# Graph attention layer: neighbouring groups of edges share their scores, their maximum and their exponentials

## What is computed

```python
h = einsum('ni,hio->hno', x, W)                       # rows of 256, and two scores of 4 per node
e = attn_src[:, src_idx] + attn_dst[:, dst_idx]
e = where(e >= 0, e, 0.2 * e) * edge_weight
e_exp = exp(e - max(e))
denom = segment_sum(e_exp, dst_idx)
out = segment_sum(h[:, src_idx] * e_exp / (denom[:, dst_idx] + 1e-10), dst_idx)
```

## Time and profile before

| | us |
|---|---|
| median of 3 runs (range) | 2468.64 (2465.61 to 2472.03) |
| the profiled execution | 2466.78 |
| its span | 2465.0 |
| start of the gathers of layer 1, from the span's start | 1695.59 |

### The profile page before, as it was taken

How to read it: one execution, slowest core, us unless ns; L and a number is a source line. 1 busy time by engine, 2 the same in 40 slices (tenths; PEclk the granted TensorE clock), 3 DMA queues, 4 the chain that set the end, 5 groups by cost and what they waited for, 6 DMA issues and landing times.

```text
span 2465.0 us, 41568 instructions
## 1 busy us (share of the span) xinstructions
PE 1989.2 (81%) x12990; PEld 1757.5 (71%) x12990; DVE 1594.8 (65%) x4240; ACT 1416.0 (57%) x2926; POOL 1473.5 (60%) x1204
## 2 busy tenths in 40 slices
PE   7799999999999999999999999945155655555560
PEld 6699889999999999989999989943144444444450
DVE  6466666666666666666666666654266566666575
ACT  2488888888888888888888888834011111111112
POOL 0327777777776777767777777423555555555503
PEclk9899999999999999999999999977567767776785
DMA  6888877777777777777777777574344544444413
GB/s 209 282 208 184 193 165 164 167 163 170 159 158 155 161 158 158 159 157 160 158 160 158 160 159 156 112 186 126 91 113 121 128 112 118 119 119 115 120 48 108
DMA packets 236177, 370.91 MB, mean 150 GB/s; under 512 B 35853, under 2 KB 168935, under 8 KB 235949
## 3 DMA queue, kind: packets, MB, share of 16 engines
q0 software_dynamic: 101232, 188.20, 38.7%
q1 hardware_dynamic: 134717, 179.94, 24.7%
HBM read 270.57 MB, written 97.45 MB: 149 GB/s over the span
## 4 chain that ended last, share of the span: by engine, by line
PE 56%; issue 18%; DVE 11%; ACT 5%; DMA 5%; another core or an unknown queue 4%; POOL 1%; SPq 0%; DVEq 0%; ACTq 0%; POOLq 0%
PE bank L1412 12%; PE bank L1410 12%; PE bank L1411 12%; PE bank L1462 4%; PE bank L1453 4%; DMA accA<-ystage,to_a 3%; PE bank L1479 2%; DVE in_window L860 2%; PE bank L1503 2%; PE bank L1514 2%; PE bank L1504 2%; PE bank L1515 2%; PE bank L1578 1%; ACT drop L1849 1%
## 5 line engine op out<-in xcount | busy, mean ns | idle before, releaser
L1306 POOL DMA_INDIRECT accA<-ystage,to_a x391 | 649.7, 1662 | 233.8 <-issue 111.6
L1312 POOL DMA_INDIRECT GA<-TA,src_c x391 | 426.7, 1091 | 323.3 <-issue 95.4
L1341 POOL DMA_INDIRECT Hg<-HT,src_c x391 | 372.9, 954 | 335.6 <-DVE xb L912 174.8
L1849 ACT ACTIVATE drop<-neg_m 128x1 f32<-128x1 f32 x98 | 28.9, 295 | 613.1 <-issue 348.2
L1410 PE MATMUL bank<-h1h,W1h 128*128 128x512 f32 x882 | 349.2, 396 | 1.5 <-DVE h1l L536 1.4
L1412 PE MATMUL bank<-h1h,W1l 128*128 128x512 f32 x882 | 348.3, 395 | 0.0
L1411 PE MATMUL bank<-h1l,W1h 128*128 128x512 f32 x882 | 347.3, 394 | 0.0
L536 DVE TENSOR_TENSOR h2l<-h2f,h2h 128x512 fp32r<-128x512 f32 (+1 forms) x294 | 202.9, 690 | 202.6 <-issue 78.9
L1607 PE MATMUL bank<-diag,ones 128*128 128x128 f32 x196 | 66.5, 435 | 306.3 <-DVE diag L896 250.2
L1617 PE MATMUL bank<-xb,in_window 128*128 128x260 f32 (+1 forms) x782 | 292.9, 542 | 1.1 <-issue 1.1
L536 DVE TENSOR_TENSOR h1l<-h1f,h1h 128x512 fp32r<-128x512 f32 x294 | 195.1, 691 | 131.3 <-ACT h1h L1686 114.2
(11 more groups left out here) (208 smaller groups left out, 5196.0 us busy)
## 6 DMA issues: line engine op xcount, KB each, us to landing
TW<-TB SPq DMA_DIRECT2D x196, 203.0 KB
ef<-in_eT SPq DMA_DIRECT2D x97, 256.0 KB
bcast_i<-in_src_row SPq DMA_DIRECT2D x97, 256.0 KB
HB<-hist SPq DMA_DIRECT2D x98, 130.0 KB
rel<-RL SPq DMA_DIRECT2D x97, 128.0 KB
rem<-RD SPq DMA_DIRECT2D x48, 256.0 KB
TB<-stB SPq DMA_DIRECT2D x24, 406.0 KB
accA<-zeros SPq DMA_DIRECT2D x4, 1677.0 KB, 13.1
```

Of the source, the lines that this page charges most:

```text
L1306: return pool.indirect_dma_start(out=table, out_offset=bass.IndirectOffsetOnAxis(ap=rows, axis=0), in_=sums, in_offset=None, compute_op=AL ...
L1312: pool.indirect_dma_start(out=GA[0:n, b % (GAR * BLOCKS_PER_GROUP), :].bitcast(f32), out_offset=None, in_=TA, in_offset=bass.IndirectOffse ...
L1341: pool.indirect_dma_start(out=Hg[0:n, slot, :], out_offset=None, in_=HT, in_offset=bass.IndirectOffsetOnAxis(ap=src_c[0:n, b:b + 1], axis= ...
```

## The change

Two neighbouring groups become a pair q of NQ = 49 pairs. One-hot matrix, scores, diagonal, spread, running maximum, `drop` and exponentials are made once for a pair, on tiles twice as wide, and `window_rows` is too. Weighing, sums, carry and store stay one for each group; the odd group of a pair is carried with `keep` alone. The ring `xb` grows from 3 to 4 groups, `hist` shrinks from 8 to 6. PAD has one bank in place of two, PTOP one in place of two, PS three in place of four, and the weights have two banks for themselves. VectorE's order in iteration q is now: weigh 2q, carry 2q-2, maximum q+1, weigh 2q+1, carry 2q-1, scores q+2, window q+1, one-hot q+3. TensorE's is: sums 2q and 2q+1, spread q+2, destination scores q+3. A part of the diff (the other functions are rewritten for pairs in the same way):

```diff
...
-        REMG = 2
-        rem = sb("rem", [P, 2, REMG * GE], bf16, s2)
-        HOTR = 4
-        hot = sb("hot", [P, HOTR, GE], bf16, s2)
-        XBR = 3
-        xb = sb("xb", [P, XBR, BLOCKS_PER_GROUP, BW], f32, s2)
-        in_window = sb("in_window", [P, XBR, BLOCKS_PER_GROUP, P], f32, s2)
+        rem = sb("rem", [P, 2, 2 * GE], bf16, s2)
+        hot = sb("hot", [P, 2, 2 * GE], bf16, s2)
+        XBR = 4
+        xb = sb("xb", [P, XBR * BLOCKS_PER_GROUP, BW], f32, s2)
+        in_window = sb("in_window", [P, XBR * BLOCKS_PER_GROUP, P], f32, s2)
         diag = sb("diag", [P, 2, P], f32, s2)
...
-        HISTR = 8
+        HISTR = 6
...
-        PAD, PTOP, PS = bank[0:2], bank[2:4], bank[4:8]
+        PAD, PTOP, PS = bank[0], bank[1], bank[5:8]
...
-        iota_p, node_p = bank[2][:, P:2 * P], bank[3][:, P:P + NT * HEADS].rearrange("p (t h) -> p t h", h=HEADS)
-        GH = BLOCKS_PER_GROUP * HEADS
-
-        def weight_p(g):
-            return bank[2][:, 2 * P + g % XBR * GH:2 * P + (g % XBR + 1) * GH].rearrange("p (k h) -> p k h", h=HEADS)
+        iota_p, node_p = bank[2][:, 0:P], bank[2][:, P:P + NT * HEADS].rearrange("p (t h) -> p t h", h=HEADS)
+        QH = 2 * BLOCKS_PER_GROUP * HEADS
+
+        def weight_p(q):
+            return bank[3 + q % 2][:, 0:QH].rearrange("p (k h) -> p k h", h=HEADS)
...
+            def one_hot(q):
+
+                n = edges_of_group(2 * q) + edges_of_group(2 * q + 1)
+                dve.wait_ge(s_rem[q % 2], 16 * (q // 2 + 1))
+                if q >= 2:
+                    dve.wait_ge(s_ad, q - 1)
+                dve.tensor_scalar(hot[:, q % 2, 0:n], rem[:, q % 2, 0:n], p_f[:, :], None, ALU.is_equal).then_inc(s_hot, 1)
+
...
+            def window_rows(q):
+
+                if q >= 2:
+                    dve.wait_ge(s_S, 2 * (q - 1))
...
+            def edge_scores(q):
+
+                blocks = blocks_of_window_pair(q)
                 runs = same_rows(blocks)
-                dve.wait_ge(s_hg[g % HGR], group_arrivals(HGR, g))
-                dve.wait_ge(s_ad, g + 1)
+                dve.wait_ge(s_hg[2 * q % HGR], group_arrivals(HGR, 2 * q))
+                dve.wait_ge(s_hg[(2 * q + 1) % HGR], group_arrivals(HGR, 2 * q + 1))
+                dve.wait_ge(s_ad, q + 1)
...
-                dve.wait_ge(s_ex, g + 1)
+                dve.wait_ge(s_ex, g // 2 + 1)
...
             def carry_window(g):
 
-                dve.wait_ge(s_drop, g + 1)
-                dve.tensor_tensor(drop_k[:, g:g + 1], drop[:, g:g + 1], keep[:, g:g + 1], ALU.mult).then_inc(s_dk, 1)
+                q = g // 2
+                if g % 2 == 0:
+                    dve.wait_ge(s_drop, q + 1)
+                    dve.tensor_tensor(drop_k[:, q:q + 1], drop[:, q:q + 1], keep[:, g:g + 1], ALU.mult).then_inc(s_dk, 1)
                 dve.wait_ge(s_S, g + 1)
                 if g >= HISTR:
                     dve.wait_ge(s_hd[g % HISTR], 16 * (g // HISTR))
                 if g == 0:
                     dve.tensor_copy(hist[:, 0, 0:BW], PS[0][:, 0:BW]).then_inc(s_carry, 1)
                     return
-                dve.wait_ge(s_dk, g + 1)
+                carried = keep[:, g:g + 1]
+                if g % 2 == 0:
+                    dve.wait_ge(s_dk, q + 1)
+                    carried = drop_k[:, q:q + 1]
                 dve.wait_ge(s_carry, g)
-                dve.scalar_tensor_tensor(hist[:, g % HISTR, 0:BW], hist[:, (g - 1) % HISTR, 0:BW], drop_k[:, g:g + 1],
-                                         PS[g % 4][:, 0:BW], ALU.mult, ALU.add).then_inc(s_carry, 1)
+                dve.scalar_tensor_tensor(hist[:, g % HISTR, 0:BW], hist[:, (g - 1) % HISTR, 0:BW], carried,
+                                         PS[g % 3][:, 0:BW], ALU.mult, ALU.add).then_inc(s_carry, 1)
...
             window_scores(0)
-            for i in range(-3, NG + 1):
-                if 0 <= i < NG:
-                    weighted_rows(i)
-                if 0 <= i + 1 < NG:
-                    window_rows(i + 1)
-                    edge_scores(i + 1)
-                if i + 3 < NG:
-                    one_hot(i + 3)
-                if 0 <= i - 1 < NG:
-                    carry_window(i - 1)
-                if 0 <= i + 1 < NG:
-                    running_maximum(i + 1)
-                if i >= 0 and i % ADC == 2 and i // ADC + 1 < NG // ADC:
-                    window_scores(i // ADC + 1)
-                if i == ADC // 2:
+            for q in range(-3, NQ + 1):
+                if 0 <= q < NQ:
+                    weighted_rows(2 * q)
+                if 0 <= q - 1:
+                    carry_window(2 * q - 2)
+                if 0 <= q + 1 < NQ:
+                    running_maximum(q + 1)
+                if 0 <= q < NQ:
+                    weighted_rows(2 * q + 1)
+                if 0 <= q - 1:
+                    carry_window(2 * q - 1)
+                if 0 <= q + 2 < NQ:
+                    edge_scores(q + 2)
+                if 0 <= q + 1 < NQ:
+                    window_rows(q + 1)
+                if q + 3 < NQ:
+                    one_hot(q + 3)
+                if q >= 0 and 2 * q % ADC == 2 and 2 * q // ADC + 1 < NG // ADC:
+                    window_scores(2 * q // ADC + 1)
+                if q == ADC // 4:
                     last_rows()
...
+            def load_remainders(q):
+                a, n = 2 * q * GE, min(2 * GE, E - 2 * q * GE)
+                if q >= 2:
+                    sp.wait_ge(s_hot, q - 1)
+                sp.dma_start(rem[:, q % 2, 0:n], RD[0, a:a + n].partition_broadcast(P)).then_inc(s_rem[q % 2], 16)
+
+            for q in range(-5, NQ):
+                if q + 5 < NQ:
+                    load_remainders(q + 5)
+                if q >= 0:
+                    for g in (2 * q, 2 * q + 1):
+                        sp.wait_ge(s_carry, g + 1)
+                        sp.dma_start(HB[g * P:(g + 1) * P, :], hist[:, g % HISTR, :]).then_inc(s_hd[g % HISTR], 16)
...
+            def destination_scores(q):
+
+                pe.wait_ge(s_hot, q + 1)
+                pe.wait_ge(s_adw, 2 * q // ADC + 1)
+                if q >= 1:
+                    pe.wait_ge(s_sc, 3 * (q - 1) + 1)
+                for j, b in enumerate(blocks_of_window_pair(q)):
                     n = rows_of_block(b)
                     for part in range(3):
-                        last = pe.matmul(PAD[g % 2][0:n, j * HEADS:(j + 1) * HEADS], hot[:, g % HOTR, j * P:j * P + n],
-                                         ad_p[:, part, g, :], start=part == 0, stop=part == 2)
+                        last = pe.matmul(PAD[0:n, j * HEADS:(j + 1) * HEADS], hot[:, q % 2, j * P:j * P + n],
+                                         ad_p[:, part, b // BLOCKS_PER_GROUP, :], start=part == 0, stop=part == 2)
                 last.then_inc(s_ad, 1)
 
-            def spread_maxima(g):
-
-                pe.wait_ge(s_topc, 2 * g + 2)
-                if g >= 2:
-                    pe.wait_ge(s_mg, g - 1)
-                pe.matmul(PTOP[g % 2][:, 0:P], ones[:, :], diag[:, g % 2, :], start=True, stop=True).then_inc(s_sp, 1)
+            def spread_maxima(q):
+
+                pe.wait_ge(s_topc, 2 * q + 2)
+                if q >= 1:
+                    pe.wait_ge(s_mg, q)
+                pe.matmul(PTOP[:, 0:P], ones[:, :], diag[:, q % 2, :], start=True, stop=True).then_inc(s_sp, 1)
 
             def window_sums(g):
 
-                pe.wait_ge(s_win, g + 1)
+                pe.wait_ge(s_win, g // 2 + 1)
                 pe.wait_ge(s_xb, g + 1)
-                if g >= 4:
-                    pe.wait_ge(s_carry, g - 3)
-                for j, b in enumerate(blocks_of_group(g)):
-                    n = rows_of_block(b)
-                    last = pe.matmul(PS[g % 4][:, 0:BW], in_window[0:n, g % XBR, j, :], xb[0:n, g % XBR, j, :],
-                                     start=j == 0, stop=b == blocks_of_group(g)[-1])
+                if g >= 3:
+                    pe.wait_ge(s_carry, g - 2)
+                blocks = blocks_of_group(g)
+                for b in blocks:
+                    n, j = rows_of_block(b), b % (XBR * BLOCKS_PER_GROUP)
+                    last = pe.matmul(PS[g % 3][:, 0:BW], in_window[0:n, j, :], xb[0:n, j, :],
+                                     start=b == blocks[0], stop=b == blocks[-1])
                 last.then_inc(s_S, 1)
 
             pe.wait_ge(s_hc, NT)
             pe.wait_ge(s_x1c, NT)
-            for i in range(-2, NG):
-                if i + 2 < NG:
-                    destination_scores(i + 2)
-                if 0 <= i + 1 < NG:
-                    spread_maxima(i + 1)
-                if i >= 0:
-                    window_sums(i)
+            for q in range(-3, NQ):
+                if q >= 0:
+                    window_sums(2 * q)
+                    window_sums(2 * q + 1)
+                if 0 <= q + 2 < NQ:
+                    spread_maxima(q + 2)
+                if q + 3 < NQ:
+                    destination_scores(q + 3)
...
```

(59 more changed lines are left out.)

79 lines of the change are left out of this document (29 added, 50 removed).

## The result

The changed kernel takes 2453.45 us, median of 9 runs (2433.98 to 2462.94), the kernel before 2468.64 (9 runs): ratio 0.9924, interval 0.9906 to 0.9942. It is faster by 0.8%, 15 us where 60 were forecast. The profiled execution took 2453.26 us, its span 2451.1.

The account below looks back on a forecast made before the run. VectorE's chain set the pace, with TensorE's completions late during long gather series and GpSimd waiting for slots. Terms -157.7, +12, +88, +12, -14.5 made -60: 2407, stated as 2405 us; own range 2360 to 2445, whole range 2312 to 2495.

Parts of the forecast that it names:

- first gap of GpSimd: Start of the layer: after filling 12 slots GpSimd restarts 12 us later, against 10.9 before.
- all later stops, `window_scores` in them: Group loop: 42 times 8 gathers at 2.1 us idle, +88, and five more `window_scores` and `last_rows`, +12.
- tail: After the last gather: six pairs at 6.7 us and a last sum and carry, 44 for 58.5, so -14.5 us.
- The prediction's own sign of being wrong: Gather stretch: the prediction is wrong if GpSimd's idle time is above 157 us.
- TensorE's completions arrive within about 0.2 to 0.8 us: Group loop: once a gather series runs out, late results reach VectorE that soon; stop at the scores 4.3 us.
- from results to restart: Stop at the scores: VectorE needs scores 1.1, window 1.1, one-hot 0.5, weighing and issue 1.5, that is 4.2 us.
- the 3.7 us taken for a stop of before: Group loop of the kernel before: GpSimd waits some 3.7 us for ring slots after each series of 8 gathers.
- the 0.8 us of rows 4: Timeline of two groups before: VectorE sees the second spread's result 0.8 us after the last gather ends.
- ScalarE's wait ahead of the weighing: VectorE's path: 0.76 us of waiting for ScalarE goes, since exponentials are made one pair ahead.
- The circle stays as it was: Group loop: each 8 gathers still cost 3.3 us, lateness taking its toll by the gather; 2461 us, chance 0.12.
- A stop at the scores after every 8: Group loop: the wait moves from spread to destination scores, 4.5 us for every 8 gathers; 2520 us, chance 0.16.
- GpSimd becomes the bound: Group loop: completions prompt enough, idle only the first 12 us (-146), tail -38; 2283 us, chance 0.17.

Follow-up runs that it names:

- e6: Changed kernel with each of the 24 bf16 destination products of a pair made twice: 2495.02 us (one run).
- e1: Changed kernel with one destination product of 12 columns for three of 4, VectorE adding the parts: 2398.95 us, ratio 0.9764.
- e5: Changed kernel with sharing alone, in VectorE's and TensorE's order of before, and a third one-hot buffer: 2425.12 us, ratio 0.9823.
- e17: Changed kernel with scores still two pairs ahead, but weighings side by side and carries and maximum at the end: 2493.97 us, ratio 1.0162.
- e16: Kernel of e5 with e1's edit, one destination product of 12 columns for three of 4: 2447.83 us, ratio 0.9976.
- e3: Changed kernel with each gather from group 12 on fetching 16 rows in place of 128, results wrong: 2443.78 us (one run).
- e18: Changed kernel itself, unedited, run again on a chip where its trace shows no late TensorE results: 2254.67 us, ratio 0.987.
- e4: Changed kernel with only the first 12 groups gathered, later groups reusing those rows, results wrong: 2166.74 us (one run).
- e10: Changed kernel with every second gather left out from group 12 on, results wrong: 2189.21 us (one run).
- e7: Changed kernel with 12 more small float32 products of 4 columns ahead of each spread on TensorE: 2458.87 us (one run).
- e2: Kernel before with one destination product of 12 columns for three of 4, VectorE adding the parts: 2438.34 us, ratio 0.9935.

## Why the prediction came out wrong

What was measured, beside the terms of its sum (us):

| term | forecast | measured |
|---|---|---|
| layer's first gather | 0 | +3.0 |
| first gap of GpSimd | 12 | 8.7 |
| all later stops, `window_scores` in them | 88 + 12 | 156.2 |
| GpSimd's idle time in all, against 157.7 before | 112 | 164.9 |
| tail | 44 | 33.5 |
| total | -60 | -14 |

The gain is thus the tail's alone (25.0 us less). The stretch with the gathers grew by 7.2 us, and its start moves by several us from trace to trace (1689.3 to 1699.9). The prediction's own sign of being wrong, idle time above 157 us, came true.

**The step that failed** is "TensorE's completions arrive within about 0.2 to 0.8 us" once the series has run out, of which I took the lowest. They arrive 3.1 us after it, GpSimd stands for 6.9 to 7.0 us in place of 4.3, and 8 gathers cost 3.5 in place of 2.1: 42 x 1.4 = 59 us. The table has 56 more than forecast in that term, and the whole miss is 46. The pattern was the one forecast: of the 24 series that a stop ends, 17 have exactly 16 gathers, and 15 of these end at the scores. The rest of the step held too: from results to restart 2075.93 - 2071.83 = 4.1 us, against 4.2.

The profile of before had what was needed to size it. After a series of 8 the result came 0.8 us late. After the 56 of the start the restart took 10.9 us, far more than VectorE's 2 to 4 us behind a result, and the row between has the lateness:

```profile
1773.69 0.29 DVE L903 TENSOR_REDUCE top_g<-bank 128x1 f32<-128x128 f32 x1 [5.98 <-remote]
```

That is 1773.69 - 1765.53 = 8.2 us behind the series. Lateness after the end thus grew with the series, and I lengthened the series twofold and left it at its smallest. A straight line between the two points gives 2.0 us for 16, an estimate that would have found some 40 of the 56 us. After the fact the loops on the late chips bear the growth out, whatever the products and the order: 0 to 2.2 us behind 8 gathers (kernel before, e6), 2.4 behind 12, mostly 2.7 to 3.5 behind 16 (changed kernel, e1, e5, e6, e17), 3.7 behind 24 (e16). Only e3 with its short gathers lies higher. The first series of the layer is less regular: 4.9 us behind 48 (1763.38 - 1758.46) and 9.2 behind 64 in e16, but 2.2 behind 60 in e1.

Three smaller slips: 4.2 us and a lateness of 0.2 are 4.4, not 4.3; the 3.7 us taken for a stop of before is a long one, as most of them stood for 2.8 to 3.7; and the 0.8 us of rows 4 is one value of many that lie between 0 and 1.7.

The other terms: the tail was too dear by 10.5 us, since VectorE's pair is 6.43 us and not 6.7 (the window 1.14 from start to start, as taken), and the last pairs have no scores, windows and one-hots left to make; the first gap was 3.3 too long. ScalarE's wait ahead of the weighing is gone, as forecast.

**The rivals.** "The circle stays as it was" gave 2461 us, the nearest number, and per pair 13.48 became 13.62. That is luck: its reason, a toll by the gather whatever VectorE does, is refuted: with the same gathers the late chips show 12.55 (e5), 12.59 (e1), 14.15 (e16) and 14.54 us (e17) per pair. "A stop at the scores after every 8" comes near to what e17 has in cost, though not in pattern: mostly series of 16 with stops of 9.2 to 9.9 us, where the rival had 4.5 for every 8. All its late waits are at the scores, and it is slower than the kernel before, as the rival said. "GpSimd becomes the bound" is what happens on S and T: the mean pair is 10.00 us in e18, the first gap 1.6 and the tail 15.0. There the kernel before takes 2283 to 2285 us, so that even this case brings only 28 us (0.987), not the 184 that the rival gave it; what bounds the kernel before on such a chip no trace here shows.

**What sets the pace on the late chips.** Shown: the lateness needs gathers (e4), nearly all of it goes when they come in short series (e10), and it does not shrink with their rows (e3). The number of bf16 one-hot products hardly changes how late a result is behind 16 gathers (2.8 us in e1, 3.1 in the changed kernel, 3.3 in e6), but it changes where and how often VectorE meets it: after 16 at the maximum, after 16 at the scores, or after 8 and 16 at the scores. That place and the way back from it go with 12.6 to 14.6 us per pair, and single gains don't add (e16). For small float32 products nothing is shown (e7). On chip Q the sharing in the old order came to 0.9823, and the whole change on R and in the result to 0.9903 and 0.9924; so the new order seems to give back some of what the sharing brings there. As no late chip ran both, this is argued across chips, though per pair (12.55 against 13.56 and 13.62) it is well above what chips of that kind differ by in the kernel before (13.20 and 13.48).

**Late semaphores, and then late work.** The bursts shown above are finished work whose semaphores come late. But TensorE's recorded work does not go on in time for ever either. In the first series of the kernel before it comes nearly to a stand, though it waits for nothing that the profile shows:

```profile
1753.15 0.29 PE L1598 MATMUL bank<-ad_p,hot 128*128 128x4 bf16 x4
1755.36 0.16 PE L1598 MATMUL bank<-ad_p,hot 128*128 128x4 bf16 x1 [1.92 <-issue]
1758.16 0.16 PE L1598 MATMUL bank<-ad_p,hot 128*128 128x4 bf16 x1 [2.64 <-issue]
...
1769.36 0.17 PE L1598 MATMUL bank<-ad_p,hot 128*128 128x4 bf16 x1 [3.33 <-issue]
```

Matmuls that come singly like this stand in all traces of the late chips but those of e1, e2 and e16 with their merged products, in e3 and e6 all through the loop. None stands in the traces of S and T. It looks as if TensorE could run only so far ahead of results that it hasn't been able to tell, but no run here tests that.

**Open:** what holds the results back, and what is different about S and T. As no chip was used in a second session, the two kinds are told from one session each. Something differs before layer 1 already: from 60 to 1500 us the traces of S and T have an update for each of some 1368 recorded signals of TensorE, those of the late chips for 1007 to 1061. The Trainium skill, in "SBUF — State Buffer", section "Who interferes with whom", has it that TensorE never waits on anyone there. On S and T the trace agrees (0.02 us from end to semaphore). On the late chips TensorE does stand still and its results come late, but no row says that the SBUF is what it waits for, so the rule is neither borne out nor refuted there; it did not protect the time.

## What to carry to other kernels

When an engine waits for results that were recorded long ago, read how late they are after series of different lengths before forecasting a deeper pipeline: more run-ahead buys longer series, and the lateness behind them can eat the gain. Reorder one thing at a time, and time it together with the others, since here two gains of 1.8% and 2.4% made 0.2% together. Before giving an instruction a price, look whether it moved the place where a wait is met: in e1 nearly the whole gain was the shorter way back. And where the same kernel's time differs by several per cent from chip to chip, take a trace of the kernel before and of the changed one on each kind of chip before explaining anything.

## What the runs showed of the hardware

- The same program (the kernel before) takes 2452.7 to 2469 us on some chips and 2283 to 2285 on others, at the same full clock until 1530 us (0.99). For the changed kernel in the result and on T, 182 of the 196 us between the spans lie between the first gather and the last carry of layer 1 (2386.9 - 1698.6 against 2199.9 - 1693.3).
- On the first kind, while GpSimd issues indirect gathers every 1.25 us, a semaphore of TensorE rises 16.9 us after the recorded end in the loop (2071.71 against 2054.84) and 47.1 us at the layer's start (1763.26 against 1716.19); VectorE waits up to 15.6 us (e16) and 47.29 us for it. On the second kind it is 0.02 us.
- In the changed kernel held results come in a burst some 3 us after a series of 16 gathers, 0.09 us from one to the next.
- A gather of 16 rows is issued every 1.15 us, one of 128 rows every 1.25: nearly all of it is fixed.
- For a kernel that has to do well on both kinds, e1 (0.9764 and 0.9887) and e5 (0.9823 and 0.9863) are the best tried; the changed kernel has 0.9903 to 0.9924 on late chips and 0.987 on T.
